# Start addresses of the on-chip buffers in a decoder block: 32-byte multiples against 1 KB multiples

## What is computed

```python
x = x + attn(layernorm(x))            # 32 heads of 16, one shared k and v of 16, ALiBi, causal
x = x + cross(layernorm(x), ctx_4096) # 32 query heads of 128, 8 kv heads, RoPE, key mask
x = x + ffn(layernorm(x))             # D_FF = 1376: (silu(x @ Wg.T) * (x @ Wu.T)) @ Wd.T
```

## The kernel before, in words

| tensor | residue before | residue after |
|---|---|---|
| `hsT_hl`, `ctxT_hl`, `cross_wqkv_hl`, `cross_wo_hl`, `cross_v_hl`, `cross_qT`, `cross_kT` | 896 | 0 |
| `cross_scores`, `rotated`, `rotated_other_half` | 896 | 0 |
| `cross_probsT_hl`, `cross_outT_hl`, `last_hs_rows` | 992 | 0 |
| `ff_hT_hl`, `ff_downT_hl`, `ff_gate_upT_hl`, `ff_work` | 896 | 0 |
| `self_qT_high_above_low`, `self_k_by_head_hl`, `self_q_hl`, `xn`, `xnT` | 160 | 0 |
| `self_wq`, `self_wo` | 416 | 0 |
| `self_wkv` | 416 | 512 |
| `self_probs`; `self_probsT`; `self_attn`, `self_attnT`, `self_hs`, `ctx_tok` | 704; 736; 864 | 0 |
| `self_v_and_ones` (a sequence's rows are 68 bytes apart) | 160 | 0 |
| `x` | 384 | 0 |
| `staged_rows` | 128 | 0 |
| `ident` | 384 | 384 |

## Time and profile before

### The profile page before, as it was taken

The page is one execution under the profiler, slowest core; times in us unless marked ns, Lnnn a source line. Parts: engine busy times, 40 slices in busy tenths (PEclk is TensorE's granted clock), DMA queues, the critical chain, the costliest instruction groups (busy, mean ns, idle before and its releaser), DMA issues. The chain is left out here.

```text
span 1014.1 us, 15751 instructions
## 1 busy us (share of the span) xinstructions
PE 987.1 (97%) x5128; PEld 809.2 (80%) x5128; DVE 589.1 (58%) x973; ACT 429.5 (42%) x1239; POOL 382.2 (38%) x375
## 2 busy tenths in 40 slices
PE   5999999989999999999999999999999989999998
PEld 3877777877888888888888888888888768888787
DVE  3755566645776676666666767657666773343100
ACT  2776776761433533523533533533432543333100
POOL 7422222163562642652642643634623422222200
PEclk8999999989999999999999999999999999999999
DMA  6000000211120210210210210210200112222001
GB/s 202 13 11 11 11 10 10 63 52 52 32 63 11 54 52 0 70 33 0 72 31 0 72 31 0 73 31 11 83 1 0 33 32 66 69 68 70 10 32 42
DMA packets 49954, 39.98 MB, mean 39 GB/s; under 512 B 4128, under 2 KB 40096, under 8 KB 49920
## 3 DMA queue, kind: packets, MB, share of 16 engines
q1 hardware_dynamic: 49536, 38.48, 12.8%
q0 software_dynamic: 384, 1.05, 0.3%
HBM read 37.43 MB, written 2.10 MB: 39 GB/s over the span
## 5 line engine op out<-in xcount | busy, mean ns | idle before, releaser
L624 PE MATMUL bank<-cross_wo_hl,cross_outT_hl 128*128 128x512 f32 x768 | 191.7, 398 | 1.0 <-POOL cross_wo_hl L618 0.6
L624 PE MATMUL bank<-hsT_hl,cross_wqkv_hl 128*128 128x512 f32 x768 | 188.2, 394 | 0.0
L624 PEld LDWEIGHTS bank<-cross_wo_hl,cross_outT_hl 128*128 128x128 f32 x768 | 143.1, 188 | 35.6 <-POOL cross_wo_hl L618 1.6
L624 PEld LDWEIGHTS bank<-hsT_hl,cross_wqkv_hl 128*128 128x128 f32 x768 | 141.9, 188 | 29.3
L938 ACT ACTIVATE cross_scores<-cross_scores,cross_negmax 128x128 f32<-128x128 f32 x256 | 99.8, 391 | 127.1 <-DVE cross_negmax L876 127.1
L798 POOL TENSOR_TENSOR cross_qT<-rotated,rotated_other_half 128x512 f32<-128x512 f32 x64 | 82.8, 1293 | 161.8 <-DVE rotated_other_half L840 161.8
L624 PE MATMUL bank<-hsT_hl,ff_gate_upT_hl 128*128 128x512 f32 (+1 forms) x528 | 120.4, 390 | 2.7 <-DVE ff_gate_upT_hl L1140 2.7
L624 PEld LDWEIGHTS bank<-hsT_hl,ff_gate_upT_hl 128*128 128x128 f32 (+1 forms) x528 | 97.7, 185 | 25.0 <-DVE ff_gate_upT_hl L1140 3.1
L948 ACT CAST cross_outT_hl<-bank 128x512 fp32r<-128x512 f32 x64 | 37.1, 580 | 143.3 <-PE bank L624 142.4
L838 DVE TENSOR_TENSOR rotated<-bank,cosT 128x512 f32<-128x512 f32 x80 | 55.2, 690 | 71.2 <-PE bank L624 71.1
L624 PE MATMUL bank<-ctxT_hl,cross_wqkv_hl 128*128 128x512 f32 x384 | 94.2, 394 | 1.1 <-PEq L74 1.1
(11 more groups left out here) (117 smaller groups left out, 1539.7 us busy)
## 6 DMA issues: line engine op xcount, KB each, us to landing
staged_rows<-in_wq SPq DMA_DIRECT2D x32, 256.0 KB, 2.8
staged_rows<-in_wo SPq DMA_DIRECT2D x32, 256.0 KB, 2.7
staged_rows<-in_wg SPq DMA_DIRECT2D x10, 256.0 KB, 2.9
staged_rows<-in_wu SPq DMA_DIRECT2D x10, 256.0 KB, 2.9
staged_rows<-in_wd SPq DMA_DIRECT2D x10, 256.0 KB, 2.9
ctx_tok<-in_ctx SPq DMA_DIRECT2D x8, 256.0 KB, 2.6
staged_rows<-in_wk SPq DMA_DIRECT2D x8, 256.0 KB, 3.0
staged_rows<-in_wv SPq DMA_DIRECT2D x8, 256.0 KB, 3.1
```

The costliest lines, as they stand in the source:

```text
L624: i = nc.tensor.matmul(out, stationary[:, a], moving[:, b], start=(first and k == 0), stop=(last and k == 2))
```

## The change

No instruction is added, removed or moved. In the self-attention the small tensors are allocated behind the large ones; in the cross attention three small ones (`negmax`, `rowsum`, `rinv`) move behind the large ones; in `program` the small ones and `ident` move ahead of `staged_rows`, with 128 unused bytes between.

```diff
+PAD = 32
@@ self_attention
         bias = sb("alibi_bias", [P, HEADS, P])
-        rel = sb("relative_position", [P, P])
-        head_of_row = sb("head_of_row", [P, QUAD])
         wq = sb("self_wq", [P, KT, DM])
         wo = sb("self_wo", [P, KT, DM])
-        wkv = sb("self_wkv", [P, KT, 2 * HD1])
         wk8 = sb("self_wk_8_times", [P, KT, 8, HD1])
-        stats = sb("self_stats", [P, 2, 6])
...
         q_hl = sb("self_q_hl", [P, STEPS, 2, QUAD * HD1], F32R)
         qT = sb("self_qT_high_above_low", [P, STEPS, P], F32R)
-        kT = sb("self_kT_8_times_hl", [P, 2, P], F32R)
         kexp = sb("self_k_by_head_hl", [P, 2, 2, QUAD, P], F32R)
-        v = sb("self_v_and_ones", [P, SEQS, HD1 + 1])
         S = sb("self_scores", [P, 2, QUAD, P])
         PR = sb("self_probs", [P, 2, QUAD, P])
-        negmax = sb("self_negmax", [P, 2, QUAD])
...
         ctx_tok = sb("ctx_tok", [P, DM])
+        kT = sb("self_kT_8_times_hl", [P, 2, P], F32R)
+        rel = sb("relative_position", [P, P])
+        wkv = sb("self_wkv", [P, KT, 2 * HD1])
+        v = sb("self_v_and_ones", [P, SEQS, HD1 + 1])
+        rsum = sb("self_rsum", [P, HEADS])
...
@@ cross_attention
         S = sb("cross_scores", [P, 2, QUAD, P])
+        PT = sb("cross_probsT_hl", [P, 2, QUAD * P], F32R)
+        oT = sb("cross_outT_hl", [P, 2, 2, QUAD * P], F32R)
+        last_hs = sb("last_hs_rows", [P, EARLY, DM])
         negmax = sb("cross_negmax", [P, 2, QUAD])
         rowsum = sb("cross_rowsum", [P, 2, QUAD])
         rinv = sb("cross_rinv", [P, 2, QUAD])
-        PT = sb("cross_probsT_hl", [P, 2, QUAD * P], F32R)
-        oT = sb("cross_outT_hl", [P, 2, 2, QUAD * P], F32R)
-        last_hs = sb("last_hs_rows", [P, EARLY, DM])
@@ program
+        m = {
+            "exponent": sb("minus_half_and_eps", [P, 2]),
+            "norm_stats": sb("norm_stats", [P, 6]),
+            "norm_mv": sb("norm_mean_var", [P, EARLY + SEQS, 2]),
+            "norm_rstd": sb("norm_rstd", [P, EARLY + SEQS, 2]),
+            "ident": sb("ident", [P, P]),
+        }
+        sb("up_to_a_multiple_of_1_KB", [P, PAD])
         stage = sb("staged_rows", [P, SLOTS, DM])
-        m = {
+        m |= {
...
-            "exponent": sb("minus_half_and_eps", [P, 2]),
...
             "x": sb("x", [P, SEQS, DM]),
-            "ident": sb("ident", [P, P]),
             "hsT_hl": sb("hsT_hl", [P, 2, KT, TOK], F32R),
```

More of the change, by code:

```diff
@@ L93, in self_attention @@
         qT = sb("self_qT_high_above_low", [P, STEPS, P], F32R)
-        kT = sb("self_kT_8_times_hl", [P, 2, P], F32R)
         kexp = sb("self_k_by_head_hl", [P, 2, 2, QUAD, P], F32R)
-        v = sb("self_v_and_ones", [P, SEQS, HD1 + 1])
         S = sb("self_scores", [P, 2, QUAD, P])
         PR = sb("self_probs", [P, 2, QUAD, P])
-        negmax = sb("self_negmax", [P, 2, QUAD])
         PT = sb("self_probsT", [P, 2, QUAD, P])
-        rsum = sb("self_rsum", [P, HEADS])
         attn = sb("self_attn", [P, DM])
@@ L105, in self_attention @@
         ctx_tok = sb("ctx_tok", [P, DM])
+        kT = sb("self_kT_8_times_hl", [P, 2, P], F32R)
[3 more added lines that the diff above has]
+        rsum = sb("self_rsum", [P, HEADS])
+        mv0 = sb("x_mean_var", [P, SEQS, 2])
+        rstd0 = sb("x_rstd", [P, 2, SEQS])
+        stats = sb("self_stats", [P, 2, 6])
+        head_of_row = sb("head_of_row", [P, QUAD])
+        negmax = sb("self_negmax", [P, 2, QUAD])
+        mv = sb("x1_mean_var", [P, 2])
+        rstd = sb("x1_rstd", [P, 2])
         pos = sb("positions", [P, SEQS], I32)
@@ L1280, in program @@
             "norm_rows": stage[:, 3:5, :],
-            "exponent": sb("minus_half_and_eps", [P, 2]),
-            "norm_stats": sb("norm_stats", [P, 6]),
-            "norm_mv": sb("norm_mean_var", [P, EARLY + SEQS, 2]),
-            "norm_rstd": sb("norm_rstd", [P, EARLY + SEQS, 2]),
             "x": sb("x", [P, SEQS, DM]),
-            "ident": sb("ident", [P, P]),
             "hsT_hl": sb("hsT_hl", [P, 2, KT, TOK], F32R),
```

## The result

| | median | lowest to highest | runs |
|---|---|---|---|
| before | 1015.9 us | 1015.5 to 1017.31 | 5 |
| changed | 1010.08 us | 1008.7 to 1010.83 | 5 |

The ratio is 0.994, with a 95% interval of 0.9926 to 0.9955: faster by 0.6%, 5.8 us. The profiled execution of the changed kernel took 1010.83 us with a span of 1009.0.

A forecast was written before the change was run, and what follows sets the result against it. PE was taken to bound the kernel, through the time from one matmul to the next. Gains of 4.2 + 0.6 + 1.3 + 0.6 + 0.3 = 7.0 us took 1015.9 to 1008.9 us, range 1007.0 to 1011.3, widened to 1005.5 to 1013.0.

The forecast's parts named there:

- the ends 0.9, 1.9 and 0.9: High ends of three gains in us: output products behind plain matmuls, probability products, projections behind an output product.
- What bounds the kernel: Whole kernel: PE is busy 987.1 of 1014.1 us, so only its matmul distances or a new wait can move the time.
- Output products: Cross attention: 49 behind F32R products gain 0.085 us each, 4.2 us; 15 behind plain matmuls 0.04 each, 0.6 us.
- Probability products and projections behind output products: Cross attention: 64 probability products gain 0.02 us each, 1.3 us; 42 projections 0.015 each, 0.6 us.
- Does the gain reach the end?: PE's one wait in a group, for L901, stays 0.23 us and takes nothing of the gain.
- the sum of 6.6 us: Forecast shrinkage of the distance from 275 us to the end of the cross attention.
- The self-attention's scores: Self-attention: both operands at 160; the second distance of a pair may lose some ns, 0.3 us in all.
- The assumption that 0 behaves like 896 because both are multiples of 64: All F32R operands: residue 0 is as good as 896 and 384; 992 and 160 are not multiples of 64.
- No change: Output and probability products: the surcharge comes from something else they share, such as ACT and DVE writes; 1015.9 us, 9%.
- Slower: Projections and feed-forward: residue 0 has the rate of 992, costing 1,944 matmuls 13.8 us; 1029.7 us, 5%.
- the 1 KB boundary: All 2,904 F32R matmuls: crossing one boundary fewer gains 6 ns each, 17.4 us; 991.5 us, 5%.

The follow-up runs named there:

- theory E: The two starts of a product must agree modulo 256 bytes; tried on the changed kernel with gaps of 256, 512, 768 and, in one product, 192: 1012.53 us.

## Why the prediction was right, and where it was wrong

1008.9 us was forecast, 1010.08 measured, inside the forecast's own range of 1007.0 to 1011.3. Of the 7.0 us of gain 5.8 came, since the scores gave nothing of their 0.3 and a wait took 0.3; the rest is within what the clock early in the kernel moves between executions. In the range, the ends 0.9, 1.9 and 0.9 stand without a working, and the low end keeps three terms at their middles.

*What bounds the kernel.* Right: PE's distances were the time. 6.2 us shorter in the stretch of the output products, 5.1 us in the whole execution.

*Output products.* 0.085 us each forecast; 2.80 - 2.72 = 0.08 behind a projection, 2.88 - 2.83 = 0.05 behind scores (0.04). Right.

*Probability products and projections behind output products.* 0.02 and 0.015 us forecast, 0.02 and 0.02 measured, the second rounded up from 0.01 (2.730 to 2.720 us in the median of 42). Right, and so was the reading that a projection needs two matmuls to come to the low rate: its first distances behind an output product were 232 and 231 ns, then 227.

*Does the gain reach the end?* Nearly: the waits for L902 grew from 1.6 to 1.9 us, eight and not seven. In the other kernels, too, they are eight and 1.8 or 1.9 us where the operands of all output products agree, and seven and 1.6 where none do. I had said that the wait takes nothing. With it the sum of 6.6 us for this stretch comes to 6.3, against 6.2 measured.

*The self-attention's scores.* Wrong: 0.3 us forecast, but a pair takes 131.80 - 131.25 = 0.55 us as before, in these rows of the changed kernel:

```profile
131.25 0.71 PE L499 MATMUL bank<-self_k_by_head_hl,self_qT_high_above_low 128*128 x2
131.80 0.60 PE L509 MATMUL bank<-ident,self_probs 128*128 128x128 f32 x4
```

Both operands stood at 160, and so agreed before as they do now; by theory E there was nothing to gain. The cross attention begins 1.2 us later in the profiled execution (its first projection at 236.3 us against 235.1), but 1.0 us later too in the kernel with the self-attention of before. It is the clock: 0.75 of the 1.2 us have arisen by 14 us and 1.12 by 28 us, while the same five matmuls of L442 take 2.74 us before and 3.47 in the changed kernel, some of them at half the rate. First before, then changed:

```profile
11.39 2.74 PE L442 MATMUL bank<-self_wq,xnT 128*128 128x512 f32 x5
13.97 1.05 PE L448 MATMUL bank<-xnT,self_wk_times 128*128 128x128 f32 x8
...
27.37 0.60 PE L508 MATMUL bank<-ident,self_probs 128*128 128x128 f32 x4
```

```profile
11.41 3.47 PE L443 MATMUL bank<-self_wq,xnT 128*128 128x512 f32 x5
14.72 1.05 PE L449 MATMUL bank<-xnT,self_wk_times 128*128 128x128 f32 x8
...
28.49 0.60 PE L509 MATMUL bank<-ident,self_probs 128*128 128x128 f32 x4
```

*The assumption that 0 behaves like 896 because both are multiples of 64.* This is the step that failed, although its number held. The kernel with everything at 32 needs no more than 227 ns a matmul. The rows shown ahead of the prediction admitted the other reading: in both products that paid, the operands disagreed (992 against 896), and in all that didn't, they agreed modulo 256 (896 against 896 or 384). I saw two tensors at an odd place and put the blame on the place. For this change both readings give the same kernel and the same time, so it was luck that the wrong one did no harm. They part for the next one: by mine, one would pad every tensor to 64 bytes and could keep 128 between the two operands of a product, which cost the projections in the run with gaps of 64 and more some 5 ns a matmul; that kernel as a whole is slower than the one before (ratio 1.0051).

*The rivals.* "No change", by "SBUF — State Buffer", "Specifications (TRN2)", of the Trainium skill: lines of 16 bytes, which all starts respected before and after. The runs disagree: 16-byte differences cost 7 or 3 ns and 32-byte ones 6. The rival's own mechanism, the writes of ACT and DVE, is out too: from 965 us on, in the down product, ACT and POOL do nothing and DVE writes only `x`, at 0 in both kernels, yet the 32-byte gap took its distances from 227.3 to 232.8 ns. "Slower" by a bad residue 0, and "the 1 KB boundary": neither; 0, 32, 64 and 896 have the same 389 ns. "TensorE: Matmul & The Clock Gate" of the Trainium skill, "Part 2: What happens when you issue a matmul", gives the loads and the streams read ports of their own, so that one takes nothing from the other; a distance that depends on their relative start, between 227 and 234 ns, speaks against that in this case, though the runs don't settle where they meet.

## What to carry to other kernels

Where F32R matmuls with a 128x128 stationary operand and 512 columns run back to back, see to it that the stationary and the moving operand of each product start at the same place modulo 256 bytes; it was worth 3% of such a matmul, and its sign in the profile is a median duration of 392 to 397 ns beside 389, or a distance of 230 to 234 beside 227. Put all such products at one place while at it: in the kernels with 389 ns in every product they all stood at one place modulo 256, and a short product beside disagreeing ones paid though its own operands agreed. A small tensor allocated between two large ones is enough to lose it, and one moved line to get it back; an absolute alignment achieves it only because it makes all places equal. When two classes of equal instructions differ, vary the suspected property in one operand and in both, before the rule is written down.

## What the runs showed that I had not expected

- The period is 256 bytes, the common place doesn't matter, and 8 bytes of difference are enough to cost 3 ns of 227. Plain float32 matmuls show nothing of it: `self_wo` at 416 against `self_attnT` at 864, a difference of 192 modulo 256, has the 592 ns that it has with both at 0, and the same distance, 429 ns.
- The cost hangs on several matmuls together and not on one alone. With agreeing operands the distances settle at 226, 227, 227 ns; with a difference of 96 they go round in 231, 234, 235, 233, 232, 237, 238 and don't settle within the 12; one disagreeing matmul in three spoils one or two distances. A projection whose operands agree settles behind a disagreeing output product after two distances in the kernel before, after four with both low parts shifted, and at once with one of them shifted.
- The spread between executions comes in good part from the clock early on. Stretches of the changed kernel from 20 to 27 and from 27 to 40 us (columns as in the earlier trace rows), and of the one with everything at 64:

```profile
20.00:27.00 7.00, 5.19 (x17) 3.33 (x16) 6.30 (x12) 4.50 (x14) 6.20 (x11) 0.54 0.00 0
27.00:40.00 13.00, 12.72 (x85) 10.24 (x83) 9.20 (x18) 8.35 (x24) 8.30 (x14) 0.98 0.08 21
```

```profile
20.00:27.00 7.00, 4.81 (x21) 3.12 (x22) 5.78 (x11) 3.84 (x11) 6.20 (x12) 1.00 0.00 0
27.00:40.00 13.00, 12.70 (x96) 10.91 (x94) 11.12 (x23) 10.00 (x29) 10.37 (x16) 1.00 0.08 21
```

  From 20 to 27 us PE works mostly at the lower level, 1.2 GHz, in the changed kernel (granted 0.54), and at 2.4 in the other (1.00), whose cross attention begins at 234.7 and not 236.3 us. No layout decides this: with the places of the changed kernel and only the low part of the stationary operands shifted, the stretch also has 1.00 and the cross attention begins at 234.6 us; and of the changed kernel's own five executions the fastest, 1008.7 us, has a mean clock of 0.995, the others 0.992. The 1.6 us are over a quarter of what the change brings. In the kernels with everything at 32 bytes, with 32-byte differences, with those under 32 and with the moving low part shifted, another such stretch falls behind the cross attention, on the first matmuls of the feed-forward (with everything at 32 bytes the granted clock is 0.76 from 822 to 829 us). It costs 1.6 and 1.5 us in the two of them where no surcharge lies over it.
